# Layer 0 of a graph network: source scores kept in the gathered rows as two parts of the rounded format, and spread over the nodes in one product

## The reference

```
h = relu(layernorm(x))
xp = (h @ W).reshape(N, 4, 256)
a_src = einsum(xp, att_src);  a_dst = einsum(xp, att_dst)       # [N, 4 heads]
e = leaky_relu(a_src[src] + a_dst[dst], 0.2)                    # edges, and one loop per node
m = segment_max(e, dst);  ee = exp(e - m[dst]);  z = segment_sum(ee, dst)
out = segment_sum(xp[src] * (ee / z[dst]), dst) + bias;  x = x + relu(out)
```

## Time and profile before

| | |
|---|---|
| median of 3 runs | 2128.14 us |
| the profiled execution | 2124.55 us |
| its span, first to last instruction | 2122.9 us |
| mean granted clock of TensorE | 0.843 |
| PE, PEld, DVE, ACT, POOL busy | 80%, 44%, 59%, 19%, 47% |
| moved by DMA | 561.66 MB, 265 GB/s |

### The profile page before, as it was taken

The page is one execution under the profiler, slowest core; times in us unless marked ns, Lnnn a source line. Parts: engine busy times, 40 slices in busy tenths (PEclk is TensorE's granted clock), DMA queues, the critical chain, the costliest instruction groups (busy, mean ns, idle before and its releaser), DMA issues. The chain is left out here.

```text
span 2122.9 us, 28347 instructions
## 1 busy us (share of the span) xinstructions
PE 1703.2 (80%) x10618; PEld 944.3 (44%) x10618; DVE 1255.3 (59%) x2915; ACT 399.4 (19%) x792; POOL 1006.3 (47%) x933
## 2 busy tenths in 40 slices
PE   3796989777278779888878788447998989989996
PEld 2443444343144445454444454213544545545454
DVE  5999999997247676676766667523433333333331
ACT  1111211111012212211221221112221222222221
POOL 1010101011556676566656663057765666767640
PEclk9897989888577787678677777668999999999898
DMA  7222223221699999999999996289998999999971
GB/s 224 87 81 66 82 82 99 81 78 55 229 378 346 349 344 368 361 338 355 356 334 340 350 359 222 86 324 396 369 359 321 360 353 347 353 356 359 339 250 45
DMA packets 175491, 561.66 MB, mean 265 GB/s; under 512 B 33805, under 2 KB 38788, under 8 KB 174990
## 3 DMA queue, kind: packets, MB, share of 16 engines
q0 software_dynamic: 128128, 416.72, 54.5%
q1 hardware_dynamic: 43618, 129.89, 18.0%
q10 hardware_dynamic: 3600, 13.16, 1.8%
HBM read 554.35 MB, written 53.70 MB: 286 GB/s over the span
## 5 line engine op out<-in xcount | busy, mean ns | idle before, releaser
L1041 POOL DMA_INDIRECT ring<-layer_rows,idx x360 | 403.1, 1120 | 239.8 <-PE acc L1166 122.3
L1616 POOL DMA_INDIRECT ring<-layer_rows,idx x360 | 366.9, 1019 | 185.3 <-issue 91.8
L542 PE MATMUL mm<-w_sb,hT 128*128 128x512 f32 x800 | 365.9, 612 | 0.0
L1166 PE MATMUL acc<-ring,weight 128*32 128x256 f32 (+1 forms) x3600 | 331.3, 482 | 7.5 <-issue 4.2
L446 POOL DMA_INDIRECT src_lists<-run,starts x28 | 55.5, 1982 | 438.5 <-DVE run L777 430.2
L1678 PE MATMUL acc<-ring,weight 128*32 128x512 f32 x1600 | 208.0, 624 | 39.1 <-issue 28.6
L542 PEld LDWEIGHTS mm<-w_sb,hT 128*128 128x128 f32 x800 | 154.8, 199 | 176.7 <-issue 176.7
L1778 DVE TENSOR_TENSOR hT_low<-tp_l,hT_high 128x512 fp32r<-128x512 f32 x50 | 34.6, 691 | 319.0 <-issue 221.2
L1166 PEld LDWEIGHTS acc<-ring,weight 128*32 128x32 f32 (+1 forms) x3600 | 149.5, 136 | 129.1 <-issue 86.4
L1711 PE MATMUL mm_l<-w_high,hT_high 128*128 128x512 f32 x400 | 171.0, 427 | 7.8 <-issue 5.8
L1238 DVE TENSOR_REDUCE highest<-wide 128x4 f32<-128x512 f32 x125 | 85.3, 682 | 149.6 <-PE wide L1133 71.5
(11 more groups left out here) (252 smaller groups left out, 2382.1 us busy)
## 6 DMA issues: line engine op xcount, KB each, us to landing
layer_rows<-row_l ACTq DMA_DIRECT2D x25, 514.0 KB, 4.1
layer_rows<-row_l SPq DMA_DIRECT2D x25, 514.0 KB
own<-layer_rows SPq DMA_DIRECT2D x25, 512.0 KB
x<-xb SPq DMA_DIRECT2D x25, 512.0 KB
x1t<-x SPq DMA_DIRECT2D x25, 512.0 KB
xt<-in_x_dram SPq DMA_DIRECT2D x24, 512.0 KB
xb<-in_x_dram SPq DMA_DIRECT2D x24, 512.0 KB
out_dram<-y SPq DMA_DIRECT2D x24, 512.0 KB
```

Source lines behind the costliest of these rows:

```text
L542: last = pe.matmul(mm[k][:, f * HALF:(f + 1) * HALF], hT[k][:, c, :], w_sb[:, c, f * HALF:(f + 1) * HALF], start=c == 0, stop=c == KC - 1)
L1041: pool.indirect_dma_start(out=ring[:, t % 2, blocks(c), :][:, q, :], out_offset=None, in_=table0, in_offset=bass.IndirectOffsetOnAxis(ap=i ...
L1166: last = pe.matmul(acc[t % 2][k * n:(k + 1) * n, h, :], by[:, k, h, :], ring[:, t % 2, blocks(c), h * C:(h + 1) * C][:, k, :], start=c == ...
L1616: pool.indirect_dma_start(out=fetched(t, c)[:, q, :], out_offset=None, in_=table1, in_offset=bass.IndirectOffsetOnAxis(ap=idx, axis=0), bo ...
```

## The change

The source scores are stored twice over in the row: first rounded to the short product format (float32r, in which PE needs one record for a product), then as the difference of the score and its rounded part. A row has 1032 floats, 4128 bytes (`ROW0`). Both parts go through the copy, the turn and the copy back (`edge_a`, `score_T` and `spread` have 32 rows or columns in place of 16), `score_T` and `spread` are in the rounded format, and `spread` has a second one in each column, so that one product adds both parts. `find_logits` first adds the two parts. `score` writes the rounded part with its copy, waits for it, and writes the difference. The two matrices are made by two comparisons each.

```diff
-        row = [sb(f"row_l0_{k}", [P, ROW]) for k in range(2)]
+        row = [sb(f"row_l0_{k}", [P, ROW0]) for k in range(2)]
...
-                act.wait_ge(scores_kept, 3 * i + 3)
+                act.wait_ge(scores_kept, 4 * i + 4)
...
-                dve.tensor_copy(row[k][:, D:ROW], asd[k][:, 0, :]).then_inc(scores_kept, 1)
+                dve.tensor_copy(row[k][:, D:D + H].bitcast(F32R), asd[k][:, 0, :]).then_inc(scores_kept, 1)
+                dve.wait_ge(scores_kept, 4 * i + 3)
+                dve.tensor_tensor(row[k][:, D + H:ROW0], asd[k][:, 0, :], row[k][:, D:D + H], ALU.subtract)\
+                    .then_inc(scores_kept, 1)
...
-        ring = sb("ring0", [P, 2, BLOCKS, ROW])
+        ring = sb("ring0", [P, 2, BLOCKS, ROW0])
...
-        edge_a = sb("edge_a", [P, BLOCKS, H])
-        score_T = sb("score_T", [QW * H, RC, P])
-        spread = sb("spread", [QW * H, H, P])
-        spread_last = sb("spread_last", [QP * H, H, P])
+        edge_a = sb("edge_a", [P, BLOCKS, 2 * H])
+        score_T = sb("score_T", [2 * QW * H, RC, P], F32R)
+        spread = sb("spread", [2 * QW * H, H, P], F32R)
+        spread_last = sb("spread_last", [2 * QP * H, H, P], F32R)
...
-                act.activation(edge_a[:, blocks(c), :], ring[:, t % 2, blocks(c), D:ROW], ACT.Copy)\
+                act.activation(edge_a[:, blocks(c), :], ring[:, t % 2, blocks(c), D:ROW0], ACT.Copy)\
...
-                n = H * (QW if c < OWN else QP)
+                n = 2 * H * (QW if c < OWN else QP)
...
-                then(dve.tensor_tensor(logit[:, :, :], edge_a[:, :, :], looked[:, :, 0:H], ALU.add), edge_a_used)
+                then(dve.tensor_tensor(logit[:, :, :], edge_a[:, :, 0:H], edge_a[:, :, H:2 * H], ALU.add), edge_a_used)
+                then(dve.tensor_tensor(logit[:, :, :], logit[:, :, :], looked[:, :, 0:H], ALU.add), math)
...
-            dve.tensor_scalar(spread_last[:, :, :], spread_last_i, 0.0, None, ALU.is_equal).then_inc(consts, 1)
-            dve.tensor_scalar(spread[:, :, :], spread_i, 0.0, None, ALU.is_equal).then_inc(consts, 1)
+            for at, to, from_i, n in ((0, spread_last, spread_last_i, 2 * QP * H), (1, spread, spread_i, 2 * QW * H)):
+                second = weight[0:n, at, :].rearrange("r (h n) -> r h n", h=H)
+                then(dve.tensor_scalar(second, from_i, float(-H), None, ALU.is_equal), math)
+                dve.scalar_tensor_tensor(out=to[:, :, :], in0=from_i, scalar=0.0, in1=second, op0=ALU.is_equal,
+                                         op1=ALU.add).then_inc(consts, 1)
```

More of the change, by code:

```diff
@@ L57 @@
 ROW = D + 4
+ROW0 = D + 2 * H
 BLK = 392
@@ L126, in build @@
     list_d = dram("src_lists", [NWP * REGION, 1])
-    table0 = dram("layer0_rows", [NP, ROW])
+    table0 = dram("layer0_rows", [NP, ROW0])
     table1 = dram("layer1_rows", [NP, ROW])
@@ L945, in attend @@
         block = ctx.enter_context(nc.Block())
-        spread_i = own[0:QW * H, 0:H * P].bitcast(I32).rearrange("r (h n) -> r h n", h=H)
-        spread_last_i = own[0:QP * H, H * P:2 * H * P].bitcast(I32).rearrange("r (h n) -> r h n", h=H)
+        spread_i = own[0:2 * QW * H, 0:H * P].bitcast(I32).rearrange("r (h n) -> r h n", h=H)
+        spread_last_i = own[0:2 * QP * H, H * P:2 * H * P].bitcast(I32).rearrange("r (h n) -> r h n", h=H)
         def blocks(c):
@@ L1024, in _ @@
             pool.iota(spread_i.rearrange("r h (q n) -> r h q n", q=QW),
-                      pattern=[[1, H], [H, QW], [0, WIN]], base=0, channel_multiplier=-1).then_inc(spread_set, 1)
+                      pattern=[[1, H], [2 * H, QW], [0, WIN]], base=0, channel_multiplier=-1).then_inc(spread_set, 1)
             pool.iota(spread_last_i.rearrange("r h (q n) -> r h q n", q=QP),
-                      pattern=[[1, H], [H, QP], [0, PAIR]], base=0, channel_multiplier=-1).then_inc(spread_set, 1)
+                      pattern=[[1, H], [2 * H, QP], [0, PAIR]], base=0, channel_multiplier=-1).then_inc(spread_set, 1)
             pool.iota(q_iota[:, :, :], pattern=[[1, QW], [0, 2 * H]], base=0, channel_multiplier=0)\
```

## The result

The changed kernel takes 2093.51 us (median of four runs, 2091.44 to 2105.46), the kernel before in its own runs beside it 2126.73: a ratio of 0.985, 95% interval 0.982 to 0.988. By that ratio it is 31 us faster. The profiled execution took 2095.53 us, 29.0 less than the one of before (2124.55).

The account below looks back on a forecast made before the run. The prediction took VectorE to bound the projection and DMA transfers the attention loop. Its terms, 5.0 + 1.2 - 6 - 2 - 3 + 1 = -3.8 us, gave 2124 us, range 2098 to 2140.

Parts of the forecast that it names:

- The projection: Score step on VectorE: copy, wait and new difference add 0.20 us for each of 25 tiles, with no cover: +5.0 us.
- Rows, copies and constants: Rows of 4128 for 4112 bytes: +1.2 us; ACT and PE copies and turn, and VectorE's spread constants: nothing.
- The spread itself: PE's spread: four records a round for eight, 0.55 us less at full clock and 0.98 at half.
- The loop: Attention turns: PE saves a mean 1.5 us in each of 23 turns, of which 17% reaches the time: -6 us.
- 17%: Attention loop: share of a change in PE's part (round 3's landing to POOL's issue) that reaches the turn; gathers absorb the rest.
- five long turns against fifteen: Trace of before: five turns with PE's part 16.1 us average 31.4, fifteen with 13.4 average 31.0; read as transfer-bound.
- Tiles 0 and 1: Start of the attention, 600 to 660 us: ten quicker spreads before the loop is full: -2 us.
- The end: End of the attention, from 1294 us: five quicker spreads of tiles 23 and 24 on the path, partly covered: -3 us.
- The added sum: VectorE's extra sum in the logits: 6.8 us over 25 tiles, mostly covered by PE's landing wait: +1 us.
- PE sets the turn: Rival: PE bounds the attention loop, which gives 35 us instead of 6: 2095 us, chance 0.15.
- The short form no quicker: Rival: one rounded record on 128 columns takes as long as two, so the gains vanish: 2135 us, chance 0.12.
- VectorE's additions all paid: Rival: PE waits for VectorE's weights in every tile, 14.7 us come on top with nothing back: 2143 us, chance 0.10.

Follow-up runs that it names:

- longer rows: The kernel before with rows of 4128 bytes, the 16 added bytes being zeros nobody reads: 2121.19 us, ratio to before 0.9989.
- pass alone: The kernel before with scores and spread matrix in the rounded format, four records a round, no second part, rows of 4112 bytes: 2009.44 us, ratio to before 0.9866.
- no spread: The changed kernel with the spread's four records of each round left out, the absent-edge record kept: 2006.95 us, ratio to before 0.9857.
- first altered order: The changed kernel with round 2 added up before PE turns round 3 of the next tile: 2086.04 us, ratio 0.981; again 1991.57 us, 0.980.
- rest alone: The changed kernel with its spread kept in plain float32, eight records a round, all else kept: 2033.89 us, ratio to before 1.0007.
- twice: The changed kernel with every spread done twice, four more records a round: 2039.29 us, ratio to before 1.002.
- all twice: The kernel before with the spread's eight records done twice in every tile from 4 to 24: 2256.19 us, ratio to before 1.063.
- some twice: The kernel before with the spread's eight records done twice in tiles 4, 8, 12, 16, 20 and 24 only: 2155.23 us, ratio to before 1.017.
- altered orders: The changed kernel with PE's row sums of rounds 2 and 3 moved in the loop, three variants: ratios to before 0.981 (again 0.980), 0.9993 and 1.011.
- before with a transfer more: The kernel before with one more DRAM-to-DRAM transfer of 0.5 MB a tile on SP's queue: 2131.98 us, ratio to before 1.0066.

## Why the prediction was wrong

**The projection, +5.0 us: right in size, wrong in cover.** From 64 to 550 us VectorE is busy for 447.38 us, 4.0 more than before. But its waits shrank in return, to be laid beside the earlier trace rows:

```profile
DVE stats L621 <- DMA xt<-in_x_dram: 11.5, 5, 7.7
DVE prod L640 <- ACT row_l L488: 3.0, 1, 3.0
```

3.0 us of the added work went under the wait for input tiles, which I had quoted beside "and for nothing else" and yet allowed no cover. The first gather came 1.8 us later in this pair and 3 us over all profiles, not 5. The instructions are as worked out: the copy starts at 325.18, the difference at 325.38, the next one at 325.46; from the copy's start that is 0.28 us, where it was 0.07, so 0.21 more for my 0.20.

```profile
325.18 0.16 DVE L650 CAST row_l<-asd 128x4 fp32r<-128x4 f32 x1
325.38 0.16 DVE L652 TENSOR_TENSOR row_l<-asd,row_l 128x4 f32<-128x4 f32 x1
325.46 1.28 DVE L621 BATCH_NORM_STATS2 stats<-xt 128x6 f32<-128x512 f32 x2
```

**Rows, copies and constants, +1.2 us and nothing: right as far as it can be told.** Longer rows alone lie between -7 and +2 us, all of the rest together costs -3 to +6.

**The spread itself: right.** 0.66 and 1.11 us for the 0.60 and 1.09 taken, and 1.0 to 1.42 us off PE's part for 1.5.

**The loop, -6 us: this is the step that failed.** The share of 17% at which I let PE's saving reach the turn was wrong; it is nearly one. In the pair of profiles PE's part lost 1.42 us and the turn 1.33 to 1.36, 27.1 us over the 20 turns; against the kernel before with longer rows PE's part lost 1.0 us and the turn 0.9, 18 us. I had read two things wrongly.

One is the DMA share of 1.00, which I took for a full queue. It is the time of all packets divided by 16 and by the stretch, and at times more than 16 packets are under way, so that a surplus at one time hides a lack at another. In the 20 turns of before the packets fall short of 16 by 0.88 us a turn (in time of all 16 engines) and exceed 16 by 0.75; in after it is 0.22 and 0.83. The runs order themselves by the share: 1.02 in after, pass alone, no spread and the first altered order, 1.01 in rest alone, 1.00 in before and twice, 0.96 and 0.85 in the slowed ones. The mean over the stage hides where the hole is. Cut into stretches, one turn of before, from the landing at 886.69 that the earlier trace rows ends its long turn with, to the next at 918.95:

```profile
886.69:899.69 13.00, 11.67 (x65) 7.12 (x65) 8.26 (x15) 4.88 (x9) 7.39 (x8) 0.50 1.01 397
899.69:904.69 5.00, 5.00 (x40) 2.81 (x40) 4.00 (x13) 0.20 (x1) 0.99 (x1) 0.50 0.58 230
904.69:918.95 14.26, 12.37 (x116) 7.71 (x115) 9.01 (x23) 1.11 (x7) 9.33 (x10) 0.86 1.02 337
```

and the same stretches of one turn of after:

```profile
883.50:896.50 13.00, 10.59 (x88) 5.71 (x88) 9.31 (x23) 5.22 (x10) 9.05 (x8) 0.71 1.02 400
896.50:901.50 5.00, 4.68 (x35) 2.52 (x38) 4.59 (x13) 0.50 (x3) 3.17 (x4) 0.66 0.94 337
901.50:913.40 11.90, 6.33 (x78) 3.86 (x70) 5.83 (x16) 0.65 (x3) 8.14 (x8) 0.92 1.04 318
```

Thirteen us after this landing the DMA engines of before run short of work, because PE has not yet freed round 3's place: 0.58 for 5 us. This turn of before is the one with the longest PE's part of all (16.92 us), so the hole is at its plainest in it. In the turn of after it is 0.94. Counted over all transfers of 20 turns, the packets under way short of 16 make 0.88 us a turn in before, 0.64 with longer rows, 0.52 in rest alone, 0.22 in after, 0.26 in no spread, 0.81 in twice and 6.15 in all twice. What remains of the turn is 30.2 us in before, 29.5 in after, 29.6 in no spread and 30.0 in twice. So half of the 1.36 us is the hole that closed. What the other half is stays open. The model that goes with most runs is a hinge: with PE's part under about 12.5 us the turn is 29 to 30 us, above it the turn grows by 0.6 to 0.9 of what PE's part does (some twice, all twice and twice 0.6 to 0.8, before against after 0.9). Rest alone and longer rows lie above it, with turns of 30.7 us at 13.1 and 13.4, and the altered orders bend it below.

The other is the experiment that I saw in the trace of before, five long turns against fifteen, 31.4 and 31.0 us for 2.7 us of PE's part. Counted again from the landings and POOL's issues, the 20 turns hold four with a long PE's part (15.9 to 16.9 us), not five; they average 16.2 us and the turn 31.7, the other sixteen 13.2 and 31.0. That is 0.7 of 3.0 us, a quarter. And the turns of that trace range from 29.3 to 33.1 us, with a standard deviation of 0.9 to 1.0, so that a difference between four and sixteen of them is uncertain by 0.5: within twice that, what I called 17% could have been over 50%. It was not 100%, and why those four were as short as they were remains open; the long turns that I made (some twice) were each 5 us longer for 7 to 8 us of PE's part. One of the four is the turn above, of 32.26 us, with the hole plainly in it, had I cut it open.

**Tiles 0 and 1, -2 us:** +2.1 in this pair of profiles. But the profile of before is short in this piece: four other kernels that do the same there as it does (longer rows, before with a transfer more, some twice, all twice) have 126.8 to 127.7 us, for its 119.29, and the changed kernel has 121.37 here and 120.3 and 121.3 in two more profiles of groups in which before took 2119 us or more. So the pair's +2.1 is most likely chance, and the change gained some 6 us here; the 27.1 us of the 20 turns are then too many by that much or more. In the two quicker groups of runs the piece shows no such gain (113.6 us in rest alone, 113.8 in the changed kernel). **The end, -3 us:** -7.5, or -6 beside the longer rows. Of the 7.5, 3.6 us lie between the landings of round 3 of the last two tiles (23.60 and 20.02 us), a turn that I had counted in the loop. Why the end shrank by more than the 4.0 us of spreads that I had put on its path is open.

**The added sum, +1 us:** not resolved (-3 us when taken away, overlapping intervals).

**The rivals.** "PE sets the turn" gave 2095 for 0.15, and the result is 2093.5: paying PE's saving nearly in full was the right price for this change, though the runs bound it. That the sum comes out to 1.5 us is partly luck: it had 35 us in the loop, where 18 to 27 in 20 turns were measured, and too little in tiles 0 to 2 and at the end. It holds about as far as the changed kernel goes: the next 1.3 us off PE's part, by leaving the spread out, were worth nothing that the intervals can tell. "The short form no quicker" fell with the 0.66 us. "VectorE's additions all paid" fell with PE's waits on weights, 0.6 us in all for 2.8 before:

```profile
PE acc L1171 <- DVE weight L1279: 0.6, 2, 0.3
```

I wrote that the 17% was the likeliest way to be wrong, and still let the forecast built on it carry 0.63 of the chance.

## What to carry to other kernels

A mean DMA share of one over a stage does not say that transfers alone bound it; cut one turn into stretches of a few microseconds and look for the hole, and who issues late there. If there is one, what shortens the work ahead of the late issue was paid nearly in full here until the hole was closed; after that, leaving more work out brought nothing, while another order of the same work still brought 0.7 us a turn. A correlation between parts of the same turn is weak evidence for what a lasting change will do: the standard deviation of the turns says how weak.

## What the runs showed of the hardware

- The rounded format spreads 128 columns in four records in 0.66 us at full and 1.11 at half clock, against 1.15 and 2.07 for the eight of plain float32, at 32 rows as at 16.
- In two of the five groups of runs before took 2035 and 2033 us, in the others and beside the changed kernel's first measurement 2119 to 2127. Most of the difference lies in layer 1: from its first gather on, the changed kernel takes 654 us in a quick group and 729 to 736 in the others, and the same stretch moves 405 GB/s in the quick group (first row) and 358 in another (second):

```profile
1400.00:1900.00 500.00, 490.73 (x2872) 268.44 (x2865) 198.70 (x485) 118.34 (x211) 383.04 (x378) 0.99 1.03 405
```

```profile
1400.00:1900.00 500.00, 454.48 (x2476) 238.64 (x2480) 174.66 (x430) 104.85 (x187) 344.45 (x334) 0.96 0.98 358
```

  Tiles 0 to 2 take 113.8 and 121.3 us, while the turns of layer 0 are as long in both (29.70 and 29.66 us). Whether this belongs to the chip is not shown: the runs record the same chip number (8) for the group of 2035 us and for a later one of 2119. Times are therefore compared by ratio to runs of before in the same group.
- Half a megabyte a tile more costs 0.6 us a tile by the medians (0.9 a turn in its profile), half a megabyte less saves 1.0 by the ratios (0.8 a turn in its profile), where 366 GB/s would make it 1.4. The engines then moved 373 and 359 GB/s, so some of it passes beside the rest.
- The busy share of the DMA engines can read 1.00 while they lack work: in before, 0.88 us a turn of fewer than 16 packets under way, and 0.75 of more than 16.
